# SyncE's order of issue in a routed feed-forward kernel: gates two jobs ahead, biases one job ahead in six buffers, the next phase's first W1 ahead of the sorted rows

## The reference

```python
xn = _layernorm(x, axis=-1)
# attention: a causal convolution with a sum of two decaying exponentials per column
out = irfft(rfft(xt, n=2*S) * rfft(k, n=2*S))[..., :S]
attn = silu(transpose(out) + xn * omega)
# feed-forward: R = 4 rounds, E = 4 experts, the best 2 of them for each row
for r in range(R):
    flat = cur.reshape(-1, h)
    logits = flat @ Wg[r] + bg[r]
    vals, idx = jax.lax.top_k(logits, TOPK)
    w = jax.nn.softmax(vals, axis=-1)
    cw = jnp.sum(one_hot(idx, E) * w[..., None], axis=1)
    hmid = gelu(einsum('nh,ehf->enf', flat, W1) + b1[:, None, :])
    y = einsum('enf,efh->enh', hmid, W2) + b2[:, None, :]
    cur = cur + einsum('ne,enh->nh', cw, y)
return x + attn + cur
```

## Time and profile before

| | us |
|---|---|
| median of 3 runs (705.14 to 710.83) | 706.83 |
| the profiled execution | 702.66 |
| its span, from the first to the last instruction | 700.8 |

### The profile page before, as it was taken

The page is one execution under the profiler, slowest core; times in us unless marked ns, Lnnn a source line. Parts: engine busy times, 40 slices in busy tenths (PEclk is TensorE's granted clock), DMA queues, the critical chain, the costliest instruction groups (busy, mean ns, idle before and its releaser), DMA issues.

```text
span 700.8 us, 11414 instructions
## 1 busy us (share of the span) xinstructions
PE 616.5 (88%) x3289; PEld 508.3 (73%) x3289; DVE 473.7 (68%) x1049; ACT 515.9 (74%) x979; POOL 412.4 (59%) x432
## 2 busy tenths in 40 slices
PE   7667999999998998999989989998999898888580
PEld 6455877888787887888778877887788776677360
DVE  4963786688864885578656876587758875795350
ACT  4668778898786877788877877886788686777550
POOL 5658438552874375536843584438568785855664
PEclk9999999999999998999999999999899999999995
DMA  8011012646886587667975689568767798658510
GB/s 240 10 55 48 15 55 87 212 165 219 310 256 254 204 304 250 224 227 253 329 268 198 250 282 283 222 218 289 238 241 251 270 307 271 237 197 305 191 60 30
DMA packets 85898, 145.92 MB, mean 208 GB/s; under 512 B 21911, under 2 KB 49486, under 8 KB 85838
## 3 DMA queue, kind: packets, MB, share of 16 engines
q1 hardware_dynamic: 79540, 133.06, 54.8%
q0 software_dynamic: 5824, 11.87, 5.3%
q10 hardware_dynamic: 474, 0.28, 0.1%
HBM read 37.42 MB, written 12.09 MB: 71 GB/s over the span
## 4 chain that ended last, share of the span: by engine, by line
PE 50%; DVE 12%; POOL 10%; issue 9%; DMA 8%; ACT 5%; SPq 3%; another core or an unknown queue 1%; POOLq 1%; DVEq 1%; ACTq 0%
PE z L1383 8%; PE y L1399 8%; PE y L1401 7%; PE z L1385 7%; PE y L1400 7%; PE z L1384 7%; PE spare L1308 4%; POOL sorted_rows L754 4%; DVE h_lo L1216 3%; DMA w_job<-w_all 3%; POOL state L740 3%; DMA sorted_rows<-rows,position_i 3%; ACT z L889 2%; ACT h_hi L892 2%; PE misc L1330 2%
## 5 line engine op out<-in xcount | busy, mean ns | idle before, releaser
L1216 DVE TENSOR_TENSOR h_lo<-z,h_hi 128x512 fp32r<-128x512 f32 (+1 forms) x428 | 251.6, 597 | 132.6 <-ACT h_hi L892 99.1
L889 ACT ACTIVATE z<-z,b_job 128x512 f32<-128x512 f32 (+1 forms) x364 | 212.2, 583 | 102.9 <-PE z L1385 76.5
L892 ACT CAST h_hi<-z 128x512 fp32r<-128x512 f32 (+1 forms) x428 | 221.4, 517 | 13.5
L740 POOL TENSOR_TENSOR state<-state,weighted 128x512 f32<-128x512 f32 (+1 forms) x103 | 115.6, 1122 | 130.0 <-DVE weighted L1163 128.1
L1399 PE MATMUL y<-h_hi,w_job 128*128 128x512 f32 (+1 forms) x364 | 134.7, 370 | 22.6 <-DVE h_lo L1216 13.8
L1383 PE MATMUL z<-cur_hi,w_job 128*128 128x512 f32 (+1 forms) x364 | 139.3, 383 | 13.4 <-DMA w_job<-w_all 10.3
L754 POOL DMA_INDIRECT sorted_rows<-rows,position_i x112 | 118.2, 1055 | 32.6 <-issue 22.4
L1400 PE MATMUL y<-h_lo,w_job 128*128 128x512 f32 (+1 forms) x364 | 130.1, 357 | 0.0
L1401 PE MATMUL y<-h_hi,w_job 128*128 128x512 f32 (+1 forms) x364 | 129.9, 357 | 0.0
L1384 PE MATMUL z<-cur_lo,w_job 128*128 128x512 f32 (+1 forms) x364 | 129.8, 357 | 0.0
L1385 PE MATMUL z<-cur_hi,w_job 128*128 128x512 f32 (+1 forms) x364 | 129.4, 356 | 0.0
(11 more groups left out here) (164 smaller groups left out, 791.9 us busy)
## 6 DMA issues: line engine op xcount, KB each, us to landing
w_job<-w_all SPq DMA_DIRECT2D x182, 512.0 KB
gate_bc<-gate_rows SPq DMA_DIRECT2D x72, 256.0 KB
rows<-sorted_rows SPq DMA_DIRECT2D x28, 266.0 KB, 3.7
gate_bc<-gate_rows SPq DMA_DIRECT2D x35, 128.0 KB
out_dram<-x_tok SPq DMA_DIRECT2D x8, 256.0 KB, 5.5
sorted_rows<-rows,position_i POOLq DMA_INDIRECT x112
b_job<-b_all SPq DMA_DIRECT2D x91, 2.5 KB
rows<-in_L_ffn_W_dram SPq DMA_DIRECT2D x4, 256.0 KB, 7.5
```

The lines of the kernel that those rows point to most:

```text
L740: pool.tensor_tensor(state[job.g][:, cols_at], before, weighted[:, j % TR, 0:job.n], ALU.add).then_inc(added, 1)
L889: nc.scalar.activation(zs, zs, ACT.Gelu_apprx_tanh, bias=bias).then_inc(gelu_done, 1)
L892: nc.scalar.copy(h_hi[:, s % ZR, 0:job.n], zs).then_inc(hi_act, 1)
L1216: dve.tensor_tensor(h_lo[:, s % ZR, 0:job.n], zs, hs.bitcast(F32), ALU.subtract).then_inc(lo_done, 1)
```

## The change

SyncE's loop is written anew. The register load of the expert is now made for each of the three copies separately, instead of once a job. The biases get a ring of six. In the iteration of job j the order becomes: W1(j), W2(j), biases(j+1), gate(j+1). At the first job of a phase it is biases, W1, `load_sorted`, W2, biases(j+1), and no gate. At the second job `gates_out` and three gates follow: those of the first, the second and the third job. In the last job of a phase there are no biases and no gate. In the dense phase the gate of job j goes out in iteration j. `load_sorted` has lost its place in the tables and always comes in the first iteration of its own phase, behind the wait for that phase's table. `store_x` is placed by `ADD_AT` in place of `T_AT`. The other engines change only in the slot and the count that they wait for.

```diff
+BR = 6
-    "scatter": (19, ..., 42), "load": 45}
+    "scatter": (19, ..., 42)}
...
-        b_job = sb("b_job", [P, WR, FC + 1])
+        b_job = sb("b_job", [P, BR, FC + 1])
...
+            def job_expert(job):
+                return from_table(job.p, job.i if job.kind == "F" else 8 + job.i, E - 1)
+
+            def job_bias(j):
+                if j >= DENSE + BR:
+                    sp.wait_ge(combined, j - BR + 1)
+                sp.dma_start(b_job[:, b_slot(j), :],
+                             b_all[:, bass.ds(job_expert(JOBS[j]), 1), :].rearrange("p o f -> p (o f)")
+                             ).then_inc(job_b_in[b_slot(j)], 16)
+
+            def job_w1(j):
                 n = (j - DENSE) % WR
+                e = job_expert(JOBS[j])
                 if j >= DENSE + WR:
                     sp.wait_ge(z_full, FC * (j - WR + 1))
...
+            def job_w2(j):
+                n = (j - DENSE) % WR
+                e = job_expert(JOBS[j])
                 if j >= DENSE + WR:
                     sp.wait_ge(y_full, j - WR + 1)
...
-                if j >= DENSE + WR:
-                    sp.wait_ge(combined, j - WR + 1)
-                sp.dma_start(b_job[:, n, :], b_all[:, bass.ds(e, 1), :].rearrange("p o f -> p (o f)")
-                             ).then_inc(job_b_in[n], 16)
...
-            for j in range(NJ + 1):
-                if DENSE <= j < NJ:
-                    job_weights(j)
-                if j > 0:
-                    job = JOBS[j - 1]
-                    if job.kind == "D" and job.e == 0:
+            for j, job in enumerate(JOBS):
+                if job.kind == "D":
+                    if job.e == 0:
                         gates_out(("G", 0, job.b))
-                    if job.kind == "F" and job.i == 0:
-                        gates_out(("G", job.p, 0))
+                    broadcast_gate(j)
+                    continue
+                last_of_phase = j + 1 == NJ or JOBS[j + 1].p > job.p
+                if j == DENSE:
+                    sp.wait_ge(w_lo, 2 * E)
+                    sp.wait_ge(b_ready, 2)
+                if job.turn == 0:
+                    sp.wait_ge(table_ready, 3 * job.p)
+                    job_bias(j)
+                job_w1(j)
+                if job.turn == 0:
+                    load_sorted(job.p)
+                job_w2(j)
+                if not last_of_phase:
+                    job_bias(j + 1)
+                if job.turn == 1:
+                    gates_out(("G", job.p, 0))
                     broadcast_gate(j - 1)
-                for p in SORT_GATE:
-                    if j == LOAD_AT[p] // FC + 1:
-                        load_sorted(p)
+                    broadcast_gate(j)
+                if job.turn > 0 and not last_of_phase:
+                    broadcast_gate(j + 1)
                 for b in range(B):
-                    if j == T_AT["A", b] // FC + 3:
+                    if j == ADD_AT["A", b] // FC + 3:
                         store_x(b)
```

More of the change, by code:

```diff
@@ L107 @@
     "places": (17, 18), "pairs": (22, 22), "order": 22, "pick": 27, "jobs": 31, "table": 35,
-    "scatter": (19, 20, 20, 20, 21, 23, 24, 24, 25, 27, 31, 33, 35, 35, 40, 42), "load": 45}
+    "scatter": (19, 20, 20, 20, 21, 23, 24, 24, 25, 27, 31, 33, 35, 35, 40, 42)}
 DENSE_PHASE = {
@@ L117 @@
     "places": (31, 33), "pairs": (44, 45), "order": 45, "pick": 47, "jobs": 51, "table": 55,
-    "scatter": (34, 34, 34, 36, 36, 38, 41, 41, 42, 43, 45, 46, 47, 47, 49, 53), "load": 54,
+    "scatter": (34, 34, 34, 36, 36, 38, 41, 41, 42, 43, 45, 46, 47, 47, 49, 53),
     "stats": (-4, -4, 8, 9, 3, 4, 5, 6), "rsqrt": (10, 10, 11, 11), "apply": (-4, 1, 14, 15, 12, 13, 12, 15),
@@ L211 @@
 JOBS_AT, TABLE_AT = sort_steps("jobs"), sort_steps("table")
-SCATTER_AT, LOAD_AT = sort_steps("scatter"), sort_steps("load")
+SCATTER_AT = sort_steps("scatter")
 MISC = [(place, "logits", name) for name, place in L_AT.items()]
@@ L384, in ema_and_routed_ffn_kernel @@
         job_w2_in = [sem(f"job_w2_in{n}") for n in range(WR)]
-        job_b_in = [sem(f"job_b_in{n}") for n in range(WR)]
+        job_b_in = [sem(f"job_b_in{n}") for n in range(BR)]
         gate_bc_in = [sem(f"gate_bc_in{n}") for n in range(GR)]
@@ L474, in uses, with b_slot, b_uses @@
             return (j - DENSE) // WR + 1
+        def b_slot(j):
+            return (j - DENSE) % BR
+        def b_uses(j):
+            return (j - DENSE) // BR + 1
         def hi_count(s, on_dve):
@@ L513, in from_table @@
                 return sp.snap(number, min_val=0, max_val=top)
-            def job_weights(j):
-                job = JOBS[j]
-                n = (j - DENSE) % WR
[L518 to L524, removed]
+            def job_expert(job):
[7 more added lines that the diff above has]
+            def job_w1(j):
+                n = (j - DENSE) % WR
+                e = job_expert(JOBS[j])
                 if j >= DENSE + WR:
@@ L885, in _ @@
                     if c == 0 and job.kind != "D":
-                        act.wait_ge(job_b_in[slot(job)], 16 * uses(j))
-                    bias = b_all[:, job.e, c:c + 1] if job.kind == "D" else b_job[:, slot(job), c:c + 1]
+                        act.wait_ge(job_b_in[b_slot(j)], 16 * b_uses(j))
+                    bias = b_all[:, job.e, c:c + 1] if job.kind == "D" else b_job[:, b_slot(j), c:c + 1]
                     act.wait_ge(z_full, s + 1)
@@ L1154, in combine @@
                 job = JOBS[j]
-                b2_col = b_all[:, job.e, FC:FC + 1] if job.kind == "D" else b_job[:, slot(job), FC:FC + 1]
+                b2_col = b_all[:, job.e, FC:FC + 1] if job.kind == "D" else b_job[:, b_slot(j), FC:FC + 1]
                 if j == 0:
@@ L1158, in combine @@
                 if job.kind != "D":
-                    dve.wait_ge(job_b_in[slot(job)], 16 * uses(j))
+                    dve.wait_ge(job_b_in[b_slot(j)], 16 * b_uses(j))
                 dve.wait_ge(y_full, j + 1)
```

## The result

| | before | after |
|---|---|---|
| median (range), us | 705.99 (702.49 to 710.83) | 718.46 (716.60 to 720.69) |
| profiled execution (span) | 702.66 (700.8) | 719.18 (717.3) |

The ratio is 1.018, with a 95% interval of 1.014 to 1.023: the changed kernel is slower by 1.8%, some 13 us. The forecast was 706, no change. Its range, 694 to 720, still holds the 718.5, near the upper end.

What follows compares the result with a forecast made beforehand. The prediction took TensorE to bound the sorted phases. Its terms, -8.1 + 4.6 - 1.0 + 1.5 + 1.0 + 0.7 + 0.5, made -0.8 us and a forecast of 706.0 us, range 694 to 720.

Steps and rivals of the forecast that it cites:

- W1 ahead, phases 2 to 7: Starts of phases 2 to 7: W1 ahead of the sorted rows ends three TensorE waits and a clock loss, -8.1 us.
- the 1.0 for the scatter: Ends of phases: W1's 512 KB go beside the scatter's last tiles and delay them, +1.0 us.
- The second rival: Starts of phases: the scatter lands later and the removed wait comes back at once, 6.4 us, total 711.4; chance 0.10.
- The entry to phase 1: Before phase 1: row loads now stand behind the table's wait and W1; TensorE waits and its clock falls, +4.6 us.
- The fourth rival: Entry to phase 1: it costs nothing, total 701.4; chance 0.07.
- Biases and gates: In the jobs: biases a job ahead end partly hidden ScalarE waits, -1.0 us; gates two jobs ahead bring 0.
- The first rival: VectorE's 12.3 us on "remote" are late gates, which gates two jobs ahead end, total 694; chance 0.17.
- Two more register loads: SyncE's jobs: 0.55 us more a job, just hidden in phases 1 to 6, costing +1.5 us in phase 7.
- the third rival: SyncE becomes the bound: W1 falls back, TensorE stands 3 us in each of seven phases, total about 726; chance 0.14.
- The store a job later: Phase 7: the last store of x goes a job later, with GpSimd's gathers behind it, +0.5 us (0 to 3).
- Three gates before W1: Second job of a phase: gates behind `gates_out` delay the third job's W1 by 1.8 us, priced at +0.7 us.
- The sum: Whole kernel: all terms added make -0.8 us, total 706.0; chance of the forecast 0.52.

Runs made afterwards that it cites:

- before_again: The kernel before, unchanged, run again in a later series for a profile: 689.15 us.
- b_loads: The kernel before with two register loads more a job, one ahead of W2 and one ahead of the biases: ratio 1.0079; with a repetition 1.0096.
- b_store: The kernel before with only the stores of x one job later: ratio 0.9999.
- b_gates: The kernel before with only the gates two jobs ahead, three of them behind `gates_out`: ratio 0.9991.
- the two pairs on the changed side: Changed kernel, one expert load, phase 1's rows early; gates ahead against gates put back: 1.0020 against 0.9982; with stores put back too, 0.9976 against 0.9938.
- b_w1_loads: The kernel before with W1 ahead of the sorted rows in phases 2 to 7 and two register loads more a job: ratio 1.0210.
- a_rows_store: The changed kernel with phase 1's rows loaded early and the stores of x at their old place: ratio 1.0166.

## Why the prediction was wrong, point by point

1. *W1 ahead, phases 2 to 7.* Held. The waits are gone in the kernel after. With the 1.0 for the scatter the forecast was -7.1; alone it measured -5.7, which is within the interval. GpSimd's addition in phase 7 (2.43 us), which the prediction didn't look at, would make the difference. The second rival, that the wait comes back at the rows, has fallen: it left 1.7 us of gain.
2. *The entry to phase 1.* Held: 4.6 forecast, 4.7 measured alone. That they agree to 0.1 is luck, with 2.1 on either side of the measurement, and on the changed kernel undoing it gave 2.9 to 5.5. The fourth rival, that the entry costs nothing, has fallen. The kernel after issues the rows at 135.60 and waits 3.54, forecast 134.4 and 3.2:

```profile
135.07 0.49 SPq L537 DMA_DIRECT2D w_job<-w_all  x1
135.60 2.72 SPq L554 DMA_DIRECT2D rows<-sorted_rows  x4
```
```profile
139.55 1.09 PE L1330 MATMUL spare<-ident,rows 128*128 128x128 f32 x4 [3.54 <-DMA rows<-sorted_rows]
```

   The window behind it has a mean clock of 0.66, between the two levels of 1.2 and 2.4 GHz, so the clock's share is there too:

```profile
139.00:144.00 5.00, 4.45 (x16) 3.73 (x17) 0.73 (x2) 2.01 (x4) 0.00 (x0) 0.66 1.11 361
```

3. *Biases and gates.* Forecast -1.0 and 0. Nothing measurable came from either (0.9938 against 0.9916 and 0.9921; 0.9991). ScalarE's waits on biases are gone in the kernel after all the same (25.6 us in before_again), so those waits were covered, as the prediction says of most of them. The gates were not free in the changed kernel: 2.6 us, twice. The first rival fell with the 17.4 us on "remote" that stayed.
4. *Two more register loads.* This is the step that failed: the term stood at +1.5 us and measured 6.6 alone, 8 to 11 in the changed kernel. The price of the loads on SyncE was right: 0.55 a job was forecast, 0.58 measured on the kernel before with only the loads. Median and count in the kernel after:

```profile
L519 SPq TENSOR_LOAD <-table_i x364: 11/275/1152, 133.4 to 672.2; - x182
```

   What failed is "in phases 1 to 6 this is just hidden", and so +1.5. The cover was taken from one job, turn 8 of phase 1, with a lead of 5.3 against one landing of 3.9. Two turns on, in phase 3 of the same trace, the lead is 4.35:

```profile
338.83 0.82 SPq L527 DMA_DIRECT2D w_job<-w_all  x1
343.18 0.39 PE L1383 MATMUL z<-cur_hi,w_job 128*128 128x512 f32 x1
```

   Nor is one landing enough. For the 61 of the 91 copies of W1 whose landing the trace has, it is, in the kernel before of the later series:

```profile
DMA to landing us min/median/max: 2.9/4.1/6.2
```

   With a landing of 5 or 6 there is nothing to spare, and in that trace TensorE waits at turn 9 or 10 of all six phases before any load is added. The prediction also let the debt grow over three jobs (1.65 against 1.4), where SyncE runs on for five: from turn 7 to turn 12 one W1 follows another after 4.3 to 4.6 us, on the mean over phases 1 to 6 of before_again. It put the cost into phase 7, where the traces have it in phases 1 to 6 (the table above). The rule of the third rival, "it decides from 0.35 a job on", would have given about the right price for the 0.55 that the forecast itself took: 4 x 0.55 - 1.4 = 0.8 us in each of seven phases, 5.6 us, next to the 6.6 measured alone. That they come so close is partly luck, since in b_loads most of the new waits are on biases, and in phase 7 there is little cost. The price of 21 us that the rival named would have needed 1.1 a job. The biases are a second path that the prediction dropped: in b_loads ScalarE waits 20 us more for them. In the changed kernel that path is closed, and the loads cost 8 to 11 us, of which 6.7 are seen as waits on `w_job` (20.0 against 13.3).

   The Trainium skill ("DMA: Bandwidth & Descriptors", Latency and other measured facts) has about 600 ns as the floor of such a load. The trace doesn't agree: the shortest load of before_again took 261 ns, and in b_loads the 91 loads ahead of W2 have a median of 0.27 us. Those ahead of the biases, with 0.69, take as long as the page says, but 600 ns is no floor here, and the measurement decides.
5. *The store a job later.* 0.5 forecast, 0 to 3 measured. The mechanism was named (GpSimd's gather behind it); the trace has its wait at 11.4 where it was 5.9, and in b_store TensorE gets half of it back at the last job.
6. *Three gates before W1.* 0.7 forecast; b_gates has -0.6 with 3 us on either side, and the two pairs on the changed side have 2.6 for all that concerns gates.
7. *The sum.* The prediction added its terms as if they lay apart. They don't: alone the parts make 6 to 9 us of the 12.5 to 15, and undone from the changed kernel loads, gates and stores each give more than they cost alone. b_w1_loads shows one such meeting, rows that wait for a W1 which SyncE reaches too late, but the changed kernel doesn't have that one. What makes up its rest of 4 to 10 us isn't shown.

The fastest version is W1 ahead alone: 0.992 of the time before, in two series.

## What to carry to other kernels

A queue that issues everything in order is a resource with a time per job, to be set against the job of the engine that it feeds: here 4.5 us against 4.2 (in phase 2 of the kernel before five jobs, four of them short, start between 241.9 and 262.8), and the 0.58 us more a job that two loads took was enough to cost 1% of the kernel. Take a cover from the leads and the landings of all jobs in the trace, with the shortest lead and the longest landing, and not from one job. Before a term is priced at nothing, look whether the trace has waits at that place already. Keep a value that several copies need in a register rather than reading it again, and when a transfer is moved ahead of a wait, ask what else it was moved ahead of.

## What the runs showed that was not expected

The kernel before took 706.0 us in the first series, 688.8 to 692.4 in four, 698.9 in the last. In the profiles of the first and last series VectorE and ScalarE have waits that end with "remote" (12.3 us of VectorE before, 17.4 of VectorE and 11.9 of ScalarE after; 15.4 and 8.7 in b_w1_loads; 9.3 and 11.7 in a_rows_store); in the profiles of the others there are none. In the first profile after, the three longest stand-stills of TensorE between the first passes of phases 1 and 7 are W2 passes that wait for `h_lo`, and each time VectorE has just waited for "remote", 4.13, 2.56 and 1.86 us. Two of them:

```profile
344.04 0.58 PE L1421 MATMUL y<-h_hi,w_job 128*128 128x256 f32 x1 [2.47 <-DVE h_lo L1238]
...
432.56 0.50 PE L1421 MATMUL y<-h_hi,w_job 128*128 128x256 f32 x1 [4.23 <-DVE h_lo L1238]
```

What makes the signals late isn't known. It comes with a time of the same program that is 1 to 2.5% longer, as much as the change did, so each version was compared with the kernel before of its own series.

One more register load a job, ahead of W2, didn't lengthen SyncE's job (4.37 against 4.47), two did by 0.58. SyncE's waits ahead of W2, for `y_full`, fell from 59.1 us to 46.2, so a part of the one load goes into them; the rest was not tested further.
